# A fused two-layer kernel: GpSimd takes every second product of a state scan's third chunk, and the order of all parts is set anew

## The reference

```python
x = _layernorm(x + _L0_attn_ref(x, ...))   # selective scan: 256 inner channels, 16 states
x = _layernorm(x + _L0_ffn_ref(x, ...))    # one quantised 128x128 layer
x = _layernorm(x + _L1_attn_ref(x, ...))   # a scan with 16 states
x = _layernorm(x + _L1_ffn_ref(x, ...))    # 8 experts, top 2, capacity 512, and a side net
```

```python
def step(h, inputs):
    dA_t, dBu_t, C_t = inputs
    h = dA_t * h + dBu_t
    y = jnp.einsum('bdn,bn->bd', h, C_t)
    return (h, y)
```

```python
gate = jax.nn.gelu(jnp.einsum('ech,ehf->ecf', h, Wg), approximate=False)
up = jnp.einsum('ech,ehf->ecf', h, Wu)
buf_out = jnp.einsum('ecf,efh->ech', gate * up, Wd) + buf
```

## Time and profile before

| | us |
|---|---|
| runs of the kernel, median | 460.06 |
| lowest and highest of 3 | 459.26, 461.53 |
| the profiled execution, its own time | 461.14 |
| its span (first to last instruction) | 459.1 |

### The profile page before, as it was taken

The page is one execution under the profiler, slowest core; times in us unless marked ns, Lnnn a source line. Parts: engine busy times, 40 slices in busy tenths (PEclk is TensorE's granted clock), DMA queues, the critical chain, the costliest instruction groups (busy, mean ns, idle before and its releaser), DMA issues.

```text
span 459.1 us, 6017 instructions
## 1 busy us (share of the span) xinstructions
PE 395.4 (86%) x1680; PEld 239.9 (52%) x1680; DVE 385.0 (84%) x848; ACT 317.5 (69%) x529; POOL 258.0 (56%) x225
## 2 busy tenths in 40 slices
PE   3979987578485799999999899999859989989993
PEld 3433422143222467776454567774225766867972
DVE  4458999999899999999999999999998755655653
ACT  3698647339773866989798998985857588666123
POOL 0019999999999644585867489767984000000000
PEclk9989999999799799999999999999997999999998
DMA  8477598796386643553644754656730000000000
GB/s 281 188 221 289 203 333 293 270 312 248 122 294 226 205 162 111 203 195 144 222 176 166 213 190 155 213 180 198 257 137 1 1 1 1 1 1 24 1 0 23
DMA packets 22064, 74.18 MB, mean 162 GB/s; under 512 B 2320, under 2 KB 4368, under 8 KB 21648
## 3 DMA queue, kind: packets, MB, share of 16 engines
q1 hardware_dynamic: 22032, 73.82, 47.0%
HBM read 72.50 MB, written 1.31 MB: 161 GB/s over the span
## 4 chain that ended last, share of the span: by engine, by line
PE 46%; issue 17%; POOL 16%; DVE 11%; ACT 7%; DMA 2%; POOLq 0%; SPq 0%; DVEq 0%; ACTq 0%
PE ps_net L718 14%; PE ps_acc L764 10%; POOL drive L1022 9%; PE ps_y L626 8%; POOL product L1051 3%; ACT L782 3%; DVE ps_state L1155 3%; PE ps_state L718 2%; DMA b_row<-bc_dram 2%; PE ps_y L764 2%; PE ps_net L591 2%; POOL delta L995 1%; PE ps_tail L640 1%; DVE acc L1335 1%; ACT ps_state L869 1%
## 5 line engine op out<-in xcount | busy, mean ns | idle before, releaser
L1022 POOL TENSOR_TENSOR drive<-du,b_row 128x512 f32<-128x512 f32 x128 | 164.3, 1305 | 24.5 <-DVE ps_state L1155 20.4
L626 PE MATMUL ps_y<-product,par 128*128 128x512 f32 x256 | 130.8, 627 | 29.0 <-DVE product L1172 21.1
L869 ACT ACTIVATE ps_state<-delta,decay_rate 128x512 f32<-128x512 f32 x128 | 84.7, 683 | 44.2 <-DVE product L1172 40.7
L626 PEld LDWEIGHTS ps_y<-product,par 128*128 128x128 f32 x256 | 46.6, 197 | 82.3 <-DVE product L1172 33.8
L782 ACT ACT_TABLE_LOAD x65 | 83.4, 1283 | 1.9 <-PEq L1409 0.7
L1051 POOL TENSOR_TENSOR product<-drive,c_row 128x512 f32<-128x512 f32 x42 | 54.2, 1290 | 35.5 <-DVE drive L1155 30.4
L1172 DVE TENSOR_TENSOR product<-ps_state,c_row 128x512 f32<-128x512 f32 x86 | 57.6, 677 | 0.6 <-issue 0.3
L764 PEld LDWEIGHTS ps_acc<-wd,hidden 128*128 128x128 f32 x448 | 53.8, 192 | 7.4 <-issue 4.3
L1155 DVE TENSOR_TENSOR_SCAN ps_state<-ps_state,drive 128x512 f32<-128x512 f32 x46 | 55.0, 1216 | 0.8 <-ACT ps_state L869 0.7
L968 ACT ACTIVATE gelu<-ps_net 128x512 f32<-128x512 f32 (+1 forms) x58 | 33.0, 595 | 32.6 <-PE ps_net L718 31.8
L764 PE MATMUL ps_acc<-wd,hidden 128*128 128x128 f32 x448 | 55.0, 276 | 0.4 <-DVE hidden L1322 0.4
(11 more groups left out here) (194 smaller groups left out, 507.1 us busy)
## 6 DMA issues: line engine op xcount, KB each, us to landing
b_row<-bc_dram SPq DMA_DIRECT2D x64, 512.0 KB, 5.0
c_row<-bc_dram SPq DMA_DIRECT2D x64, 512.0 KB, 4.1
x_in<-x_t SPq DMA_DIRECT2D x4, 256.0 KB, 6.8
gelu<-w_gate SPq DMA_DIRECT2D x1, 1024.0 KB, 9.1
hidden<-w_up SPq DMA_DIRECT2D x1, 1024.0 KB, 10.9
wd<-w_down SPq DMA_DIRECT2D x1, 1024.0 KB, 12.8
out<-acc SPq DMA_DIRECT2D x4, 256.0 KB, 2.4
par<-params SPq DMA_DIRECT2D x1, 598.0 KB, 6.5
```

The costliest lines, as they stand in the source:

```text
L626: mm(ps_y[:, :], ident, product[:, g % PRODUCTS, :], start=False, stop=(n == STATE - 1)).then_inc(y_pe, 1)
L869: nc.scalar.activation(ps_state[g % RING][:, :], delta[:, c % 2, h, :], ACT.Exp, scale=decay_rate[:, h, n:n + 1]).then_inc(decay_act, 1)
L1022: nc.gpsimd.tensor_tensor(drive[:, g % DRIVES, :], du[:, h, :], b_row[:, m % ROWS, n % 2, :], ALU.mult).then_inc(drive_pool, 1)
```

## The change

In chunk 2 of the code (the third), GpSimd multiplies the 16 odd steps in place of the 10 steps 2, 5, 8 ... 29. And the table of places is new: nearly every row of it from tail 1 on. No instruction is added or dropped; six products and six carry copies change engine, and sixteen steps are multiplied by another engine than before.

```diff
-MULTIPLIED = (QUARTER, QUARTER, THIRD, ODD)
+MULTIPLIED = (QUARTER, QUARTER, ODD, ODD)
...
     "tensor": {
...
-        "gate 2": (14.5455, 14.7071, 15.6768, 16.4848, 16.9697, 17.6162, 18.101, 19.0707, 19.2323, 19.7172, 20.3636, 20.6869, 21.6566, 21.8182, 22.6263, 22.7879, 23.7576),
+        "gate 2": (15.1919, 15.3535, 16.4848, 16.6465, 17.7778, 17.9394, 18.5859, 18.7475, 19.8788, 20.0404, 20.8485, 21.0101, 21.8182, 21.9798, 22.7879, 22.9495, 23.7576),
...
     "gpsimd": {
...
-        "settle 3": (2.069, 3.7241),
-        "du 3": (2.2069, 4.4138),
+        "settle 3": (2.3448, 3.1724),
+        "du 3": (2.7586, 5.931),
```

More of the change, by code:

```diff
@@ L145 @@
         "du 0": (18.6207, 19.1724),
[5 rows of a table removed]
[5 rows of a table added]
         "settle 2": (0.1379, 0.2759),
         "du 2": (1.2414, 6.6207),
[9 rows of a table removed]
[9 rows of a table added]
     },
     "vector": {
-        "tail 0": (0, 12.4912, 13.0526, 13.193, 14.5965, 14.8772, 15.0175, 16.8421, 18.1053, 18.386, 18.6667, 19.2281, 20.3509, 21.0526, 21.4737, 21.8947),
+        "tail 0": (0, 12.4912, 13.0526, 13.193, 14.5965, 14.8772, 15.0175, 16.5614, 18.1053, 18.386, 18.6667, 19.2281, 20.3509, 21.0526, 21.4737, 21.8947),
         "split": (0.1404, 0.2807, 0.4211, 0.5614, 0.7018, 0.8421, 0.9825, 1.1228),
         "delta 0": (1.2632, 1.4035),
[29 rows of a table removed]
[29 rows of a table added]
         "fin 3": (15.7193, 15.8596),
```

## The result

The changed kernel takes 463.56 us (median of 20 runs, 460.83 to 465.49) against 460.03 us before (20 runs, 458.82 to 461.82): ratio 1.0065, interval 1.0049 to 1.0081. It is slower by 3.5 us, where 1.5 us less was forecast (458.6), and lies outside the forecast range of 455.1 to 462.0. Four more kernels of the same text, run later as experiments, gave 1.0054 to 1.0066.

What follows compares the result with a forecast made beforehand. TensorE was taken to set the pace from 158 us, except between 311 and 353 us, where VectorE does. Terms 0 - 1.4 + 1.0 - 1.1 made -1.5 us, from 460.06 to 458.6, range 455.1 to 462.0.

Steps and rivals of the forecast that it cites:

- Before the last join of chunk 1 ... Sum: 0: TensorE ahead of up 1.16: two more parts cost 1.4 us, two removed waits give back 1.34, so no net change.
- the two waits named: TensorE's waits of 0.29 and 1.05 us around gates 1.0 and 1.1 and tail 1's counts should go: minus 1.34.
- From the last join of chunk 1 to the last scan: Four parts leave this VectorE-bound stretch, so the last scan ends 3.0 us earlier, at 350.2.
- The new wait behind gate 2.1: TensorE reaches the counts of tail 2 before VectorE has made "picked", then waits for "late": cost 1.0 us.
- The waits at the start of experts 3: TensorE's waits of 1.37 and 1.06 us for a hidden and a gelu shrink: 1.1 of 2.4 us gained.
- So by itself it is worth nothing: VectorE's 4.1 us relief from six products falls before 276 us, covered by a full TensorE; only the order cashes it.
- Up to tail 1 ... Zero, with 1 us either way.: Up to tail 1 the orders differ only by swaps of neighbours: no effect, within 1 us.
- Slower, GpSimd late at the border: Rival: seven more products before GpSimd's first drive of chunk 2 make it late, 463.6 us; chance of slower 0.14.
- Contention: Rival: nine places of VectorE work collide with GpSimd over SBUF at full price, 459.8 us; chance 0.08.
- No gain: Rival: TensorE's adds and the ring of seven products hold scans, or the wait for "picked" takes the gain, 460.1; chance 0.16.
- three signs under "Wrong": GpSimd's drives end chunk 2's first scan waits; chunk 1's last join after 312 us; end moved by TensorE idle before 158.
- signs under "Right": 48 GpSimd products, last scan near 350 us, named waits gone, 0.5 to 1 us behind gate 2.1, idle under 3.

Runs made afterwards that it cites:

- e8: The changed kernel run again without alteration, for another profile; four such repeats gave ratios of 1.0054 to 1.0066 to the kernel before.
- e2: The changed kernel with the old order of parts put back up to 158 us, new order and products behind it: 461.89 us, ratio 1.0033.
- e5: The changed kernel's new order with the old products, GpSimd making every third in chunk 2: 466.78 us, ratio 1.0145 to the kernel before.
- e3: The kernel before, in its old order, with every second product of chunk 2 on GpSimd: 468.90 us, ratio 1.0174.
- e4: The changed kernel plus seven useless 512-column products keeping TensorE busy ahead of the experts: 465.73 us, ratio 1.0084 to the kernel before.

## Why the prediction was wrong

**The step that failed** is "Before the last join of chunk 1 ... Sum: 0": B-C grew by 3.8 us (153.5 to 157.3, at full clock) in place of 0. By U and C, e8 against before, it comes apart in four:

- +1.4, the two parts more on TensorE, tail 2.2 and finish 3.6. They are the six matmuls by which B-U grew (718 to 724), as forecast.
- +0.7 of idle time of TensorE in B-U (2.3 to 3.0), where -1.34 was forecast. This term is the error, by 2.0 us.
- +1.0 more that TensorE is booked as busy in B-U (149.5 to 151.9, less the 1.4), which the forecast didn't have.
- +0.8 between U and C: the scan 3.15 ahead of the join, with its wait of 1.17 us for the decay. The forecast took this scan (1.26) off the stretch behind the join and put nothing on the side ahead of it.

Of the second: the two waits named, at 255 and 259 us, did go. But others came near them, in e8:

```profile
266.65 0.97 PE L718 MATMUL ps_net<-hn_part,wg 128*128 128x512 f32 x3 [0.18 <-DVE hidden L1322]
268.29 2.05 PE L764 MATMUL ps_acc<-wd,hidden 128*128 128x128 f32 x16 [0.66 <-DVE hidden L1322]
...
275.21 1.67 PE L718 MATMUL ps_net<-hn_part,wu 128*128 128x512 f32 x6 [0.77 <-ACT gelu L968]
```

These are 1.61 us in place of 1.74 (the 1.34, and 0.40 that stood at 268.84 before). And at 187 and 188 us, where nothing was forecast, two waits of 0.88 and 0.24 stand in place of one of 0.42:

```profile
187.25 0.96 PE L718 MATMUL ps_net<-hn_part,wg 128*128 128x512 f32 x3 [0.88 <-DVE hidden L1322]
...
188.45 1.66 PE L718 MATMUL ps_net<-hn_part,wu 128*128 128x512 f32 x6 [0.24 <-ACT gelu L968]
```

The 1.0 us inside the busy time stays open. Counted from start to start, the gates and ups take 0.8 us more in e8 than in before, and L596 and L660 0.05 us more per matmul. The same lines do so in e2 and e5, which share the new order, and not in e3, which has the old one; so it comes with the order, by what means no run shows. In e3 the busy time grew as well, by 2.8 us in B-U for the same 718 matmuls, but 1.7 of that is the half clock behind a wait.

The forecast took waits away one at a time and didn't ask which others the new order brings. Why just these come isn't shown. In B-U ScalarE is busy 2.4 us more in e8 than in before (two decays and a cast moved in), VectorE 1.0 less, and VectorE's idle time rose from 5.5 to 9.6 us.

**Right, with other sizes.** From the last join of chunk 1 to the last scan: -3.0 forecast, -3.7 measured (40.3 to 36.6), of which 0.8 is the join that came later; from U it is -2.9. The new wait behind gate 2.1: 1.0 forecast, 0.30 + 0.28 measured. The waits at the start of experts 3, 2.4 us, of which I took back 1.1, are both gone from the trace of the changed kernel. TensorE's last addition in e8 starts 41.2 us after that join instead of 44.1, 2.9 sooner (3.6 forecast), and from U only 2.1 sooner. C-D in all: -1.5 forecast, -1.9 to -2.3 measured; U-D, the fairer cut, -1.2 to -1.9. So the late half came out as forecast, but by two errors against each other: less won up to the last addition, more behind it.

**"So by itself it is worth nothing"**, of the six products, was wrong in both orders: -4.1 us in the new one, +7.6 in the old (5.9 without the clock). In the old one a scan that came sooner met a decay that didn't, and waited 2.65 us. That VectorE is busy 148 of 153.5 us suggests that it is on the path in this piece nearly as often as TensorE; no run shows how often.

**"Up to tail 1 ... Zero, with 1 us either way."** Measured A-B: 122.1 at the median of five profiles of the changed kernel, 121.2 in three of e2; 0.9 us, within that bound, and no more than the two profiles of the kernel before lie apart (121.8 and 120.9).

**The clock** was put down at 0.3 us of the low end and on the side of a gain. It can cost 2.8 us at B. The sum at full clock in B-C is A-D +2.2 us (422.5 to 424.7); the medians lie 3.5 apart, and the rest is the clock and the mixture of early and late starts, in shares that stay open.

**The rivals.** "Slower, GpSimd late at the border" gave 463.6 us, and 463.56 was measured. That is luck: its mechanism didn't come. GpSimd's first drives of chunk 3 are 7.7 us later, but the scan starts only 0.95 later, and no scan there waits for a drive. "Contention" is real and larger than the 1.0 us that the prediction gave it. In B-U VectorE makes the same operations but for the six products and six carry copies, 5.0 us that left it. Of the others, some take longer in e8 than in before (L1191, L1244, L1241, L1214 and L1207, 4.1 us together) and some less (L1247, L1261, L1136, 1.8): 2.3 us came back. What of it reached TensorE isn't shown. An operation like that, beside GpSimd's in the same profile (e8):

```profile
229.52 1.11 DVE L1191 SCALAR_TENSOR_TENSOR shift<-moments,rstd 128x4 f32<-128x4 f32 x1
...
229.34 1.27 POOL L1051 TENSOR_TENSOR product<-drive,c_row 128x512 f32<-128x512 f32 x1
```

"No gain" had a part too: in B-U of e8 VectorE's products wait 1.6 us for TensorE's additions, the ring of seven.

Of the three signs under "Wrong", the second came, the last join of chunk 1 later than 312, though not for the reason in its brackets; the third, the end moved by TensorE's idle time ahead of 158 us, isn't shown. Most of the signs under "Right" came as well (48 products, the waits near 255 to 259 and at 407 gone, 0.58 us behind gate 2.1, 2.9 us of idle time between 158 and 311), and the kernel was slower all the same: they look at the terms one by one, and none would have shown what was not in the list.

## What to carry to other kernels

Where every engine's queue is a fixed list, a piece of work that changes engine has no price of its own: here the same six products were worth -4.1 us in one order and +7.6 in another, 1.7 of it the clock. Price the products and the order together, and don't enter a removed wait of the fullest engine as a gain before you have looked for the waits that the new order brings: here 1.34 us of waits went, and the idle time in that piece still grew by 0.7. Work that you take off one stretch stands in another; put it down there too.
Cut traces at instants that don't depend on the loading before comparing them, and at instants ahead of which the same parts stand in both orders; the join C moved by 0.8 us for a scan that had been put ahead of it. And take several profiles: a single one mixed 2.8 us of clock with 2.2 us of order.

## What the runs showed of the hardware

Some small VectorE operations on SBUF wait for GpSimd's operation to end. In the pair above both end together, at 230.63 and 230.61 us; L1244 at 244.98 took 1.12 us and ended at 246.10, GpSimd's product that began at 244.81 ended at 246.08. Over all traces but e4's, 157 operations of L1191, L1241, L1244 and L1247 (128x4 elements, two inputs in SBUF) start well inside an operation of GpSimd, and 152 of them end within 0.05 us of its end; those that meet no operation of GpSimd take 0.15 or 0.16 us at the median. So the price is what is left of GpSimd's 1.3 us, not a share. Operations with an input in PSUM (L1172, 0.68 us) and the reciprocal of L1266 (one input, 0.18 us) keep their time; L1298, with one input, waits as well (17 of 17). The Trainium skill (Advanced Engine Details and Errata, VectorE Performance Modes) says that instructions of GpSimd and of VectorE's two-port modes block each other; which mode these small operations are in no run here shows.

The granted clock at the same place of the same kernel was 0.52 in one execution and 1.00 in four, in two of them behind an idle time equal to 0.01 us. The Trainium skill (TensorE: Matmul & The Clock Gate, Part 1) has the gate look at TensorE's activity at instants that don't follow the kernel; the trace agrees in so far as the same work met both levels.
